# Gated linear attention in a four-layer kernel: the order of a slot's f32 and f32r matmuls on TensorE, and of the evictions behind them

## The reference

```python
q = (x @ Wq.T).reshape(b, s, H, DH)
k = (x @ Wk.T).reshape(b, s, H, DH)
v = (x @ Wv.T).reshape(b, s, H, DH)
log_decay = -jax.nn.softplus(x @ Wd.T + bd)
gate = jax.nn.sigmoid((x @ Wg.T).reshape(b, s, H, DH))
k_gated = k * gate
# s_t = exp(g_t) * s_{t-1} + k_t^T v_t ;  o_t = q_t s_t   (per head)
out = _gla_scan(q, k_gated, v, log_decay)
out = out * rsqrt(mean(out * out, -1) + eps) * norm_w
out = out * jax.nn.sigmoid(x @ Wog.T)
return out @ Wo.T
```

## Time and profile before

| what | value |
|---|---|
| median of 3 runs | 2258.59 us (2250.94 to 2275.03) |
| profiled execution, its own time | 2256.96 us |
| its span | 2255.2 us |
| TensorE busy over the span | 2085.5 us, 92% |
| weight loads (beside matmuls) | 1476.2 us, 65% |
| VectorE / ScalarE / GpSimd busy | 1500.1 / 1286.7 / 624.2 us |
| mean granted TensorE clock | 0.949 of full speed |

### The profile page before, as it was taken

How to read it: one execution, slowest core, us unless ns; L and a number is a source line. 1 busy time by engine, 2 the same in 40 slices (tenths; PEclk the granted TensorE clock), 3 DMA queues, 4 the chain that set the end, 5 groups by cost and what they waited for, 6 DMA issues and landing times. The chain is left out here.

```text
span 2255.2 us, 41976 instructions
## 1 busy us (share of the span) xinstructions
PE 2085.5 (92%) x16626; PEld 1476.2 (65%) x16626; DVE 1500.1 (67%) x2406; ACT 1286.7 (57%) x2558; POOL 624.2 (28%) x481
## 2 busy tenths in 40 slices
PE   7999999999999928984999999999999999779998
PEld 6633333333333317973888888888888888658887
DVE  7879999999999438973445454545454544456664
ACT  3248888888888816763444444444444444345654
POOL 1200000000000004532425151515252525224444
PEclk9859999999999969995999999999999999979999
DMA  5822232322220132214203030303030303032321
GB/s 209 242 47 61 65 72 59 80 66 63 67 65 31 35 106 60 71 38 169 90 21 114 20 113 23 111 24 106 10 125 11 127 21 104 10 112 104 113 104 66
DMA packets 95657, 176.77 MB, mean 78 GB/s; under 512 B 19737, under 2 KB 57761, under 8 KB 90337
## 3 DMA queue, kind: packets, MB, share of 16 engines
q1 hardware_dynamic: 95456, 174.03, 25.2%
HBM read 134.54 MB, written 38.67 MB: 77 GB/s over the span
## 5 line engine op out<-in xcount | busy, mean ns | idle before, releaser
L572 DVE TENSOR_REDUCE att_sb_mx<-att_ps_psM 128x1 f32<-128x1024 f32 x512 | 623.9, 1221 | 36.2 <-PE att_ps_psM L605 34.0
L715 ACT ACTIVATE att_sb_pt<-att_ps_psS 128x512 f32<-128x512 f32 x1024 | 557.2, 597 | 92.4 <-PE att_ps_psS L623 37.7
L605 PE MATMUL att_ps_psM<-stack_sb_k,stack_sb_q 48*128 48x512 f32 x1024 | 389.5, 463 | 5.6 <-DVE att_sb_mx L572 4.0
L623 PE MATMUL att_ps_psS<-stack_sb_q,stack_sb_k 50*128 50x512 f32 x1024 | 381.2, 452 | 0.0
L635 PE MATMUL att_ps_psO<-att_sb_pt,stack_sb_v 128*32 128x256 f32 x4096 | 332.6, 397 | 8.6 <-ACT att_sb_osb L708 8.6
L623 PEld LDWEIGHTS att_ps_psS<-stack_sb_q,stack_sb_k 50*128 50x128 f32 x1024 | 157.1, 189 | 206.7 <-ACT att_sb_pt L715 162.1
L635 PEld LDWEIGHTS att_ps_psO<-att_sb_pt,stack_sb_v 128*32 128x32 f32 x4096 | 82.6, 109 | 196.1 <-issue 106.3
L2041 ACT ACTIVATE gla_sb_sg<-gla_ps_psP 128x512 f32<-128x512 f32 x64 | 38.3, 598 | 277.9 <-PE gla_ps_psP L1802 277.9
L2375 POOL TENSOR_TENSOR gla_sb_dm<-gla_sb_dm,gla_sb_masked 128x1024 f32<-128x1024 f32 x64 | 160.4, 2528 | 85.7 <-DMA gla_sb_dm<-decay_rows 85.7
L605 PEld LDWEIGHTS att_ps_psM<-stack_sb_k,stack_sb_q 48*128 48x128 f32 x1024 | 160.3, 193 | 20.9 <-DVE att_sb_mx L572 17.9
L2058 ACT ACTIVATE gla_sb_dm<-gla_sb_dm,gla_sb_neg_g 128x128 f32<-128x128 f32 x512 | 156.4, 391 | 6.0 <-POOL gla_sb_dm L2375 6.0
(11 more groups left out here) (250 smaller groups left out, 4774.1 us busy)
## 6 DMA issues: line engine op xcount, KB each, us to landing
gla_sb_dm<-decay_rows SPq DMA_DIRECT2D x32, 1024.0 KB, 5.6
qk_parts<-stack_sb_part SPq DMA_DIRECT2D x32, 512.0 KB, 3.3
gla_sb_eg<-decay_exp SPq DMA_DIRECT2D x64, 256.0 KB, 6.7
moe_sb_gb<-gate_rows SPq DMA_DIRECT2D x8, 2048.0 KB, 7.1
stack_sb_q<-qk_parts SPq DMA_DIRECT2D x192, 64.0 KB, 2.9
stack_sb_k<-qk_parts SPq DMA_DIRECT2D x96, 128.0 KB, 4.4
att_sb_rb<-sums SPq DMA_DIRECT2D x32, 256.0 KB
attended<-att_sb_on SPq DMA_DIRECT2D x32, 256.0 KB, 4.9
```

Of the source, the lines that this page charges most:

```text
L572: nc.vector.tensor_reduce(mx[:, qh, 8 * r + c:8 * r + c + 1], psM[:, t % 2, :], AX.X, ALU.max).then_inc(maxima_taken, 1)
L605: mm = pe.matmul(psM[:, t % 2, c * ST:(c + 1) * ST], q[rs, g, qh, j, n * P:(n + 1) * P], k[rs, g, j, c * ST:(c + 1) * ST], start=True, sto ...
L623: pe.matmul(psS[:, ring_slot(pos), :], k[rs, g, j, s * P:(s + 1) * P], q[rs, g, qh, j, :], start=True, stop=True).then_inc(ring_done, 1)
L715: nc.scalar.activation(pt[:, s % (LAG + 2), ORDER[i], :], psS[:, (pos + 1) % 3, :], ACT.Exp, scale=AD ** -0.5).then_inc(ring_taken, 1)
```

## The change

On TensorE `from_state` comes straight behind `scores(0)`, and `gate(0)` straight ahead of `key(0)`; `gate(1)` and `key(1)` follow each other, `from_chunk(0)` moves behind `keys_turned(0)`, both `from_chunk` stand together, `keys_turned(1)` follows them, and both `values` follow it. `decay_columns` and `decay_inputs` stand between `from_state` and `gate(0)`, `decay_rows_of` ahead of `gate(1)`. On ScalarE a square now comes ahead of each value copy. On VectorE `gated_keys(1)` comes ahead of `take_outputs(0)`. No instruction is added or removed, and all waits stay in their functions.

```diff
@@ tensor, slot @@
                 scores(0)
+                from_state()
+                if n == 3 and not last:
+                    decay_columns(i + 1)
+                if n == 2 and not last:
+                    decay_inputs(i + 1, 1 - u)
                 if ahead:
                     gate(*nxt, 0)
-                if n == 2 and not last:
-                    decay_inputs(i + 1, 1 - u)
-                if n == 3 and not last:
-                    decay_columns(i + 1)
-                from_state()
-                if ahead:
                     key(*nxt, 0)
                 update()
                 if n % 2:
                     out_project(c - 1)
                 scores(1)
+                if n == 3 and not last:
+                    decay_rows_of(i + 1)
                 if ahead:
                     gate(*nxt, 1)
-                if n == 3 and not last:
-                    decay_rows_of(i + 1)
-                from_chunk(0)
-                if ahead:
                     key(*nxt, 1)
                     keys_turned(nxt[0], nxt[2], 0)
-                from_chunk(1)
+                for g in range(2):
+                    from_chunk(g)
                 if ahead:
-                    values(*nxt, 0)
                     keys_turned(nxt[0], nxt[2], 1)
-                    values(*nxt, 1)
+                    for h in range(2):
+                        values(*nxt, h)
@@ scalar, slot @@
                     keys_taken(ni, nn, 0)
                     if n % 2 == 0:
                         decay_exps(ni, nu, nn, 1)
-                    take_values(ni, nn, 0)
                     keys_taken(ni, nn, 1)
-                    take_values(ni, nn, 1)
                 for g in range(2):
                     act.wait_ge(yT_ready, 2 * c + g + 1)
                     if g == 0:
                         wait_past(act, osum_ready, c if n or not first(i, 1) else 0)
                     nc.scalar.activation(osq[:, 4 * g:4 * g + 4, :], psO[:, g, :, :], ACT.Square).then_inc(osq_ready, 1)
+                    if ahead:
+                        take_values(ni, nn, g)
@@ vector, slot @@
+                if ahead:
+                    gated_keys(ni, nn, 1)
                 take_outputs(0)
                 if n % 2:
                     take_out(c - 1, n - 1, i)
-                if ahead:
-                    gated_keys(ni, nn, 1)
                 take_outputs(1)
```

## The result

| | before | changed |
|---|---|---|
| median | 2255.80 us (2242.65 to 2276.12, 22 runs) | 2240.83 us (2229.05 to 2258.65, 22 runs) |
| profiled execution, its own time | 2256.96 us | 2237.45 us |
| its span, mean granted clock | 2255.2 us, 0.949 | 2235.7 us, 0.953 |

The ratio is 0.9933, with a 95% interval of 0.9911 to 0.9956: 15 us faster, which is within 1%. The forecast was 2248.2, 7 us above the median and well inside its range. The profiled executions lie 19.5 us apart.

What follows compares the result with a forecast made beforehand. TensorE, never starving, bounds the GLA stage through the sum of distances between matmul starts. From the profiled execution, 2256.96 - 10.9 (new order) + 1.4 + 0.7 (waits) = 2248.2 us, range 2236 to 2261.

Steps and rivals of the forecast that it cites:

- the term was 0.35: TensorE's new order: each slot gains 0.42 us on projections less 0.07 among f32 products, -10.9 us over 31 slots.
- The unseen neighbourhoods: Three product pairs without a profile row: from_state and keys_turned(1) cost 0.08 us each, paired from_chunk gives back 0.09.
- f32 meeting f32r: At TensorE projections: extra matmul distance of 0.08 to 0.10 us arises where an f32 product adjoins an f32r one.
- The two waits: TensorE at keys_turned: 0.2 us on second keys in n = 0 (+1.4 us), 0.1 on decay rows in n = 3 (+0.7).
- The costs of the old places: ScalarE squares left in their old place would hold up the earlier from_state by 0.6 us each time.
- The step on the value copies: ScalarE's value copies come last in its queue, next read by update 5.9 us into the slot; cost nothing.
- I take no difference: Half-clock stretches behind decay_inputs: count taken as unchanged, with ends of -8.4 and +3.3 us.
- The price of 1.7 us a stretch: Slot with half clock behind decay_inputs: from_state to update takes 4.95 us against 3.28, so 1.7 us a time.
- B: Rival on TensorE: switch cost is only moved to f32 neighbourhoods, nothing gained, 2.1 us of waits: 2259 us; chance 0.12.
- The rule of the Trainium skill: TensorE matmul distance follows column count alone, about 216 ns for 512 columns, so the neighbour-cost term would be zero.
- C: Rival at keys_turned(1): transposes wait for VectorE in every slot, 21.7 us against 10.9 gained: 2268 us; chance 0.06.
- D: Rival: upper end of switch gains and no half-clock stretch left behind decay_inputs: 2232 us; chance 0.08.

Runs made afterwards that it cites:

- the first of the two with one stretch less: Changed kernel with gate(1) and key(1) moved directly behind key(0), each from_chunk ahead of a group of transposes, gated_keys(1) left in its place on VectorE: 2302.25 us, ratio 1.0201.

## Why the prediction was right

*Direction, size and place.* The median is inside the range and the 31 slots lost 8.8 us apart from the clock, where the sum of orders and waits gave 8.8 (10.9 less 2.1); at equal clock the runs give 10.2. That the two 8.8 agree to a tenth is luck: 0.05 us a slot more was gained than worked out, 1.6 us, and the waits cost 3.0 for 2.1. The sign "the stage shrinks by 8 to 10 us" holds for the order alone; as measured, with the clock, it shrank by 13.5. The distances did what was said: `key` starts 0.24 behind `gate`, an n = 0 takes 16.77 where the working gives 16.8, and the slots lose 0.40, 0.38 and 0.43 where the term was 0.35.

*The terms.* `gate(0)` and `key(0)` take 2.99 for the 2.97 of the working, `gate(1)` and `key(1)` 2.90 and the `values` 2.97, both as worked out. The unseen neighbourhoods: `from_state` behind `scores` +0.10 (taken 0.08), `keys_turned(1)` behind `from_chunk` +0.06 (0.08), the pair of `from_chunk` -0.16 (-0.09, and outside its bound of -0.10; both have a new neighbour on one side, and the bound allowed for one). That last one is the term that was mis-sized, and it is most of the difference between 0.35 and 0.40. It also tells which part of the change works: the middle merge is 0.35 of the 0.40, the move of `from_state` 0.00, the merge of the values 0.04. The costs were right as costs of neighbours; their reason was not. The prediction laid them to "f32 meeting f32r", and `gate(0)` behind the f32r `decay_inputs` pays the same 0.08 (1.48 for 1.40). What property of a neighbour decides stays open.

*The two waits.* In n = 0 0.2 to 0.3 us for 0.2, on the engine and line named, with keys ending 13.6 into the slot as worked out; that `from_state`'s early place is what keeps it so small was an argument in the prediction and is shown by the kernel with `gate(0)` back in front. In n = 3 0.19 for 0.1.

*The evictions.* The costs of the old places were right (0.7 for 0.6 at `from_state`, and waits at every `keys_turned(1)` without the keys' move). The step on the value copies came out right, with no wait, but for less reason than it gave: it named only `update` as their reader. The queries' projection in odd slots waits for the same copies, and only the third merge hides that (evictions alone, and `values(0)` back: 0.5 to 0.6 us in 15 slots).

*The clock.* "I take no difference" is the term that came out otherwise. In the profiles five blocks of `decay_inputs` of seven were followed by half clock before and two after (4.7 us, at 1.5 to 1.6 each), and over all the runs the change has 217.5 +- 4.2 us at half clock for the 226.6 to 230.0 (+- 3.3) of three sets of runs of before, some 11 +- 5 us less, which by the line is 4 us. Together with the 10.2 this makes the 14.3 between the means. What lowers it isn't settled: kernels with the same narrow matmuls in the same place had two, three, five, four or six of seven, and half of the difference between the two profiles (10 of 20 us at half clock) lies ahead of the stage, in code that is untouched. It may be chance. The price of 1.7 us a stretch was a little too high: the prediction set 4.95 against the 3.28 of a slot n = 0, but the same blocks take 3.37 in an n = 2 at the full clock, behind `decay_inputs`.

*The rivals.* B is refuted by the kernel with `from_chunk(0)` back: the same products with other neighbours differ by 0.35 us a slot. The rule of the Trainium skill that the prediction weighed, in "TensorE: Matmul & The Clock Gate", section "Back-to-back issue gap", has a formula for the distance that knows the column count alone; the section gives it for an isolated matmul and says that in a stream of weight loads and matmuls both set the spacing, but nothing in it depends on the neighbour. It would give that kernel the time of the changed one; the traces disagree, with 5.68 against 5.33 us for the same matmuls. C did not happen, and does at once when the second keys keep their place (TensorE's order alone), or when the transposes move nearer still (the first of the two with one stretch less). D happened by a small part. Its chance of 0.08 is less than the 0.09 given to a time that "needs D nearly whole"; the two do not fit each other.

## What to carry to other kernels

Where the tensor engine never starves, read each block as a distance from first start to first start and list what it costs beside each neighbour: here a projection of 512 columns costs 0.08 to 0.10 us more behind every other product seen than behind another projection, and 0.09 more ahead of a product that uses half of the array, and the order with the best pairs wins, not the one with the fewest stretches. Move the evictions with the matmuls, and for every eviction that becomes later ask both who reads its result and who writes its bank next, in every kind of slot: here the odd ones. When runs scatter with the granted clock, fit time against half-clock time first; it took the scatter here from some 7 us to 1.6.

## What the runs showed of the hardware that was not expected

- Over the whole program a microsecond at half clock costs 0.38 us (193 runs, twelve kernels and the one before); within the stage, where TensorE sets the time, a stretch of 3.41 us costs 1.5 to 1.6.
- 24 matmuls of 16 columns in a row, 0.11 us apart and without a gap, were followed by half clock in two to six of seven places, by kernel; 48 in a row met it in seven of seven; twice 12 with a projection between in none of fourteen (two kernels).
- A gap of PE of 1.8 to 2.4 us at the turn of the hardware loop was met by a fall of the granted clock to half, from 0.2 us ahead of the gap's end to 1.6 behind it, in eight of thirteen profiles.
- The first distance of a 512-column projection is 0.32 us behind f32r matmuls of 16 columns and behind f32 ones of 128 alike, 0.34 behind `scores`, and 0.24 behind another projection.
- Two `from_chunk` in a row, which use 64 columns of the array at a time, take 1.90 us together and 1.03 each between products that use all of it (1.03 also between two groups of transposes, all in f32).
